# Output parts, key transposes and openings of two cross-attentions put elsewhere in the order of work

## The reference

```python
kv = jnp.concatenate([context, latents], axis=1)   # layer 0; in layer 1 the context alone
q = (latents @ Wq).reshape(bsz, q_len, HEADS, HEAD_DIM).transpose(0, 2, 1, 3)
k = (kv @ Wk).reshape(bsz, kv_len, KV_HEADS, HEAD_DIM).transpose(0, 2, 1, 3)
v = (kv @ Wv).reshape(bsz, kv_len, KV_HEADS, HEAD_DIM).transpose(0, 2, 1, 3)
q = rms_norm(q, q_norm_w)
k = rms_norm(k, k_norm_w)
scores = jnp.einsum('bhgqd,bhkd->bhgqk', qg, k) * scale
probs = jax.nn.softmax(scores.astype(jnp.float32), axis=-1).astype(q.dtype)
...
return out @ Wo
```

## Time and profile before

| | |
|---|---|
| median of 3 runs | 1523.04 us (1520.77 to 1525.49) |
| the profiled execution | 1521.05 us, of which 1519.3 us are the span of the trace |
| mean granted clock of TensorE | 0.984 |
| busy: TensorE, VectorE, ScalarE, GpSimd | 1434.1 us (94%), 1013.1 (67%), 844.4 (56%), 413.2 (27%) |
| median time of a wo tile's load (1024 KB in 16) | 4.9 us |

### The profile page before, as it was taken

The page is one execution under the profiler, slowest core; times in us unless marked ns, Lnnn a source line. Parts: engine busy times, 40 slices in busy tenths (PEclk is TensorE's granted clock), DMA queues, the critical chain, the costliest instruction groups (busy, mean ns, idle before and its releaser), DMA issues.

```text
span 1519.3 us, 23906 instructions
## 1 busy us (share of the span) xinstructions
PE 1434.1 (94%) x7942; PEld 1204.3 (79%) x7942; DVE 1013.1 (67%) x1833; ACT 844.4 (56%) x1476; POOL 413.2 (27%) x570
## 2 busy tenths in 40 slices
PE   8989999988999999779999999999899999978998
PEld 6857888877888888669777788887788888756887
DVE  6778788777666667538667655567656556737765
ACT  5755767664555556426446455556555555733443
POOL 3565445432223221005126222223112222001000
PEclk9999999999999999989999999999999999989999
DMA  8455444553434343246253434344234334423242
GB/s 284 147 201 193 142 181 149 209 187 94 135 120 141 114 154 117 83 145 205 82 193 136 145 119 134 129 153 152 98 118 132 127 129 145 140 78 104 84 166 97
DMA packets 65518, 215.14 MB, mean 142 GB/s; under 512 B 16976, under 2 KB 21840, under 8 KB 58160
## 3 DMA queue, kind: packets, MB, share of 16 engines
q1 hardware_dynamic: 65424, 213.95, 41.3%
HBM read 180.76 MB, written 33.16 MB: 141 GB/s over the span
## 4 chain that ended last, share of the span: by engine, by line
PE 78%; DVE 9%; POOL 3%; ACT 3%; issue 3%; DMA 3%; SPq 0%; DVEq 0%; POOLq 0%; ACTq 0%
PE g_kbanks L54 11%; PE g_kbanks L56 11%; PE g_kbanks L55 11%; PE g_pobanks L1744 7%; PE g_vbank L54 5%; PE g_vbank L55 4%; PE g_vbank L56 4%; PE g_ktbank L1756 4%; PE g_pobanks L1730 3%; PE g_sbank L1712 3%; PE g_sbank L54 2%; PE g_sbank L55 2%; PE g_sbank L56 2%; PE g_pobanks L54 1%; DVE c_wkv_r L215 1%
## 5 line engine op out<-in xcount | busy, mean ns | idle before, releaser
L54 PE MATMUL g_kbanks<-c_wkv_r,c_cT_r 128*128 128x512 f32 x768 | 318.6, 415 | 31.4 <-DVE c_wkv_r L475 16.1
L56 PE MATMUL g_kbanks<-c_wkv_r,c_cT_r 128*128 128x512 f32 x768 | 307.4, 400 | 0.0
L55 PE MATMUL g_kbanks<-c_wkv_r,c_cT_r 128*128 128x512 f32 x768 | 307.2, 400 | 0.0
L54 PEld LDWEIGHTS g_kbanks<-c_wkv_r,c_cT_r 128*128 128x128 f32 x768 | 148.1, 193 | 64.0 <-issue 17.0
L56 PEld LDWEIGHTS g_kbanks<-c_wkv_r,c_cT_r 128*128 128x128 f32 x768 | 147.6, 192 | 34.2
L55 PEld LDWEIGHTS g_kbanks<-c_wkv_r,c_cT_r 128*128 128x128 f32 x768 | 148.0, 193 | 27.5
L1627 POOL TENSOR_TENSOR c1a_ms<-c1a_ss,c_const 128x4 f32<-128x4 f32 x64 | 12.9, 201 | 350.1 <-DVE c1a_ss L2035 350.1
L54 PE MATMUL g_vbank<-c_wkv_r,c_cT_r 128*128 128x512 f32 x256 | 100.7, 393 | 0.6 <-DVE c0a_v L2090 0.6
L55 PE MATMUL g_vbank<-c_wkv_r,c_cT_r 128*128 128x512 f32 x256 | 100.9, 394 | 0.0
L56 PE MATMUL g_vbank<-c_wkv_r,c_cT_r 128*128 128x512 f32 x256 | 100.6, 393 | 0.0
L2041 DVE TENSOR_TENSOR c0a_kn<-c0a_kn,c0a_rstd 128x512 f32<-128x512 f32 x64 | 68.8, 1074 | 47.0 <-POOL c0a_rstd L1630 47.0
(11 more groups left out here) (541 smaller groups left out, 3805.9 us busy)
## 6 DMA issues: line engine op xcount, KB each, us to landing
c_cT_r<-ctx_split_dram SPq DMA_DIRECT2D x48, 1024.0 KB, 5.5
c_cT_r<-ctx_split_dram SPq DMA_DIRECT2D x48, 768.0 KB, 4.8
ctx_split_dram<-c_cT_r SPq DMA_DIRECT2D x16, 1792.0 KB, 7.0
c_wkv<-in_l_wo SPq DMA_DIRECT2D x16, 1024.0 KB, 4.9
g_stage<-in_l_wq SPq DMA_DIRECT2D x15, 1024.0 KB, 5.2
e_stage<-in_e_w SPq DMA_DIRECT2D x20, 768.0 KB, 4.2
c_wkv<-in_l_wkv SPq DMA_DIRECT2D x16, 512.0 KB, 6.2
c_cT<-in_ctx SPq DMA_DIRECT2D x32, 256.0 KB, 3.1
```

What stands on the lines that cost most here:

```text
L54: nc.tensor.matmul(out, a[0], b[1], start=start, stop=False, skip_group_check=reopen)
L55: nc.tensor.matmul(out, a[0], b[0], start=False, stop=False, skip_group_check=reopen)
L56: return nc.tensor.matmul(out, a[1], b[0], start=False, stop=stop, skip_group_check=reopen)
```

## The change

- **Layer 0's first weights**: the sums and splits move to earlier tiles of the queries stage, T4 is summed before T3, all seven blocks are split there (before, some waited until quad 0), and a low half waits for its own sum alone. In layer 1 VectorE forms T3 at tile 13 (`first_t3`).
- **Key transposes**: `kt(2m-1, 1)` moves from the first short-step group to behind S2 T2, `kt(2m, 0)` from the second group to behind A22 T4. `place_k` and `lo_of_k` follow later in ScalarE's and VectorE's order.
- **Openings**: in the quads of the first unit and quad 2 ScalarE squares the keys behind the keep copy; `root(2m, 0)` comes before the context sums in quad 1; a context low half is made later in quad 0.
- **Finish**: each head has one output part, between the scores and pv; part 7 follows the last transposes, and parts 8 to 15 the last pv. ScalarE divides before it splits, and VectorE splits before `ot_place`.

```diff
-        dve.wait_ge(self.summed, 4)
+        block = self.FIRST[n]
+        dve.wait_ge(self.summed, self.READ_BY[block])
         dve.wait_ge(self.hi_ready, n + 1)
-        self.make_lo(self.FIRST[n], self.low(self.FIRST[n]))
+        self.make_lo(block, self.low(block))
...
-    SUM_AT = [OUTPUTS - 16 + n for n in (8, 9, 11, 12)]
-    HI_AT = [OUTPUTS - 16 + n for n in (9, 11, 13, 13, 14, 15)]
-    LO_AT = [OUTPUTS - 16 + n for n in (13, 14, 15)]
+    SUM_AT = (5, 7, 9, 11) if first else (8, 9, 11)
+    T3_AT = None if first else 13
+    HI_AT = (4, 6, 8, 10, 12, 14, 14) if first else (9, 11, 13, 13, 14, 15)
+    LO_AT = (6, 10, 12, 14, 16, 21, 22) if first else (13, 14, 15)
...
-    LATE = range(6, 7), range(3, 7)
+    LATE = (range(0), range(0)) if tail else (range(6, 7), range(3, 7))
...
+            if is_at(m, 1):
+                root(2 * m, 0)
...
                 score(*scored(u, par, side, False))
-                kt(2 * m - 1, 1)
                 pv(*summed_up(u, par, side, False), loads)
             wait_weights(kvw.T2)
             pe.wait_ge(p1_kept, m + 1)
             product(side, context.S2, kvw.T2, x_bank, False).then_inc(products, 1)
+            if not is_at(m, 0):
+                kt(2 * m - 1, 1)
...
             score(*scored(u, par, side, True))
-            kt(2 * m, 0)
             pv(*summed_up(u, par, side, True), loads)
             wait_weights(kvw.T4)
             pe.wait_ge(u3_kept, m + 1)
             product(side, context.A22, kvw.T4, x_bank, False).then_inc(products, 1)
+            kt(2 * m, 0)
...
                 score(a, UNITS - 1, 1, j)
-                out.product(pe, 2 * j + 3)
+                out.product(pe, j + 3)
                 pv(a - 1, *((UNITS - 1, 1, j - 1) if j else (UNITS - 2, 0, UNIT_H - 1)), loads)
-                out.product(pe, 2 * j + 4)
             p_transpose(LAST + UNIT_H - 1, va_added, PAIRS, zbank)
-            out.product(pe, 2 * UNIT_H + 3)
+            out.product(pe, UNIT_H + 3)
             pv(LAST + UNIT_H - 1, UNITS - 1, 1, UNIT_H - 1, loads)
-            for i in range(2 * UNIT_H + 4, PARTS):
+            for i in range(UNIT_H + 4, PARTS):
...
-            act.wait_ge(ka_added, m + 1)
-            square(2 * m, kn[:, 0, :])
-            if not is_at(m, 0):
-                place_k(2 * m - 1, 3 - 2 * side, par if side else 1 - par, u if side else u - 1)
+            opening = is_at(u, 0) or is_at(m, 2)
+            if not opening:
+                key_square(2 * m, 0, ka_added, m)
                 exponential(x1, k1)
             act.wait_ge(products, made(m, "p6"))
             need(act, va_added, m)
             nc.scalar.activation(keep[:, 0, :], x_bank, ACT.Copy).then_inc(u2_kept, 1)
+            if opening:
+                key_square(2 * m, 0, ka_added, m)
+            if not is_at(m, 0):
+                place_k(2 * m - 1, 3 - 2 * side, par if side else 1 - par, u if side else u - 1)
             divide(x1, k1)
...
-            place_k(2 * m, 2 * side, par, u)
             exponential(x2, k2)
...
+            key_square(2 * m + 1, 1, kb_kept, m)
+            place_k(2 * m, 2 * side, par, u)
             divide(x2, k2)
...
                 pt_copy(LAST + j - 1)
                 exponential(LAST + j, j)
-                out.make_hi(act, 2 * j + 4)
-                out.make_hi(act, 2 * j + 5)
                 divide(LAST + j, j)
-                for i in range(2 * j + 6, 2 * j + 8):
-                    wo.make_hi(act, i)
+                out.make_hi(act, j + 4)
+                wo.make_hi(act, j + 6)
...
                 inverse_sum(a, j)
+                out.make_lo(dve, j + 4)
+                wo.make_lo(dve, j + 6)
                 ot_place(a - 1, *((UNITS - 1, 1, j - 1) if j else (UNITS - 2, 0, UNIT_H - 1)))
-                out.make_lo(dve, 2 * j + 4)
-                out.make_lo(dve, 2 * j + 5)
-                for i in range(2 * j + 6, 2 * j + 8):
-                    wo.make_lo(dve, i)
```

More of the change, by code:

```diff
@@ L1642, in split_queries @@
             pool.wait_ge(q_hi, u + 1)
-            root(n, 0)
+            if not rooted:
+                root(n, 0)
             nc.gpsimd.tensor_tensor(flat(q[1]), mine, as_f32(flat(q[0])),
@@ L1950, in finish @@
             out.make_hi(act, 2)
+            exponential(LAST - 1, UNIT_H - 1)
             out.make_hi(act, 3)
-            exponential(LAST - 1, UNIT_H - 1)
+            divide(LAST - 1, UNIT_H - 1)
             for i in range(4, 6):
                 wo.make_hi(act, i)
-            divide(LAST - 1, UNIT_H - 1)
             for j in range(UNIT_H):
@@ L1966, in finish @@
             pt_copy(LAST + UNIT_H - 1)
-            for i in range(14, 16):
-                wo.make_hi(act, i)
-            out.make_hi(act, 12)
+            for q in range(8, 11):
+                out.make_hi(act, q)
+                if q == 10:
+                    out.make_hi(act, 11)
+                    out.make_hi(act, 12)
+                for i in range(2 * q - 6, 2 * q - 4):
+                    wo.make_hi(act, i)
             for i in range(12, PARTS):
@@ L2065, in quad @@
             total(2 * m, 0)
-            if not is_at(m, 0):
-                if tail and is_at(m, 1):
-                    dve.wait_ge(vl_stored, 32)
-                lo_of_k(2 * m - 1, 3 - 2 * side, par if side else 1 - par)
             inverse_sum(x1, k1)
@@ L2072, in quad @@
             normalise(2 * m, 0)
+            if not is_at(m, 0):
+                lo_of_k(2 * m - 1, 3 - 2 * side, par if side else 1 - par)
             late_split(1)
-            if prepared(hf, m + 1):
+            if prepared(hf, m + 1) and not is_at(m, 0):
                 context.make_lo(dve, *following(hf, b, side), 0)
             if last:
-                for i in range(2):
-                    wo.make_lo(dve, i)
+                wo.make_lo(dve, 0)
             if turning:
@@ L2090, in quad @@
             nc.vector.tensor_tensor(v[:, par, 2 * side + 1, :], zbank[:, :], keep[:, 1, :], ALU.add).then_inc(vb_added, 1)
-            if tail and is_at(m, 0):
-                dve.wait_ge(vl_stored, 32)
-            lo_of_k(2 * m, 2 * side, par)
+            if prepared(hf, m + 1) and is_at(m, 0):
+                context.make_lo(dve, *following(hf, b, side), 0)
             inverse_sum(x2, k2)
             ot_place(*summed_up(u, par, side, True))
+            if last:
+                wo.make_lo(dve, 1)
             if turning:
@@ L2105, in quad @@
             total(2 * m + 1, 1)
+            if tail and is_at(m, 0):
+                dve.wait_ge(vl_stored, 32)
+            lo_of_k(2 * m, 2 * side, par)
             dve.wait_ge(products, made(m, "p3"))
@@ L2112, in quad @@
             if last:
-                for i in range(2, 4):
-                    wo.make_lo(dve, i)
+                wo.make_lo(dve, 2)
         def finish():
@@ L2140, in finish @@
             tail_heads(LAST + UNIT_H - 1, zbank)
-            for i in range(14, 16):
-                wo.make_lo(dve, i)
-            ot_place(LAST + UNIT_H - 1, UNITS - 1, 1, UNIT_H - 1)
+            for q in range(8, 11):
+                out.make_lo(dve, q)
+                if q == 10:
+                    out.make_lo(dve, 11)
+                for i in range(2 * q - 6, 2 * q - 4):
+                    wo.make_lo(dve, i)
+                if q == 8:
+                    ot_place(LAST + UNIT_H - 1, UNITS - 1, 1, UNIT_H - 1)
             out.make_lo(dve, 12)
```

34 lines of the change are left out of this document (19 added, 15 removed).

## The result

The changed kernel takes **1508.66 us** (median of 4 runs, 1506.70 to 1511.63) against 1524.22 (4 runs): a ratio of 0.9903 (95% interval 0.9878 to 0.9929), 15.6 us faster. The forecast was 1485 with a range of 1464 to 1508: the sign was right, the size was not, and the time lies just outside. The profiled run took 1507.46 us with a span of 1505.7; before they were 1521.05 and 1519.3.

What follows compares the result with a forecast made beforehand. TensorE, busy 94%, was taken to bound the steady part, VectorE and ScalarE the finishes' heads; groups +23, openings -9 and -6, turnings -3, finishes -43 gave -38 us, hence 1485 us; range 1464 to 1508.

Steps and rivals of the forecast that it cites:

- Finishes: End of each layer's attention: one output part per head shortens the VectorE and ScalarE chain's heads, -43 us in all.
- Groups: Steady short-step groups: without key transposes TensorE waits for the probabilities' copy and lone transposes cost extra, +23 us.
- After a wait the next load follows some 0.05 sooner than in the stream: Short-step groups: queued loads gain 0.05 us after a wait, a credit taken off each group's price.
- rival A: Lone key transposes between long products are cheap, 0.34 us instead of 0.45: 1472, at best 1459; chance 0.10.
- Openings: Start of each layer's attention and the queries stage: fewer waits for keys and weight halves, -9 and -6 us.
- The kt after the next block product gets 1.4 us more, which covers the small waits: First quads: later key transposes cover small key waits, but not all of the longest, 3.3 us.
- The sums now start earlier ... TensorE waits some 4 us there: Layer 0's last queries tiles: sums at tiles 5 to 11 finish splits before the keys, against some 4 us of waits.
- The low bound of the forecast: Layer 0's opening: only 4 us gained if the conflict with GpSimd merely moves to earlier tiles.
- Turnings: Middle quads: the key wait gains a product of 1.4 us and the rest stays, -3 us (+1 to -5).
- B: Finishes stay bound by VectorE and ScalarE, each only 7 to 8 us shorter: 1513; chance 0.09.
- C: Groups: the probabilities' copy slips behind place_k, up to 0.6 us in each of 120: slower, 1557; chance 0.05.
- D: No change: finish heads stay at 9.1 us, later parts and openings pay for the steady part: 1523; chance 0.03.

Runs made afterwards that it cites:

- E9: Kernel before with the new finish and layer 1's new weight schedule, plus wo's low half made one part earlier in VectorE's gap: 1472.57 us, ratio 0.9656.
- E11: Kernel before with the new finish and layer 1's new weight schedule, but ScalarE's old order, splits ahead of the division: one run, 1472.89 us.
- E2: Kernel before with only the key transposes moved, their copies and low halves with them: 1552.31 us, ratio 1.0188.
- E7: E4 with ScalarE squaring the keys ahead of the keep copy in the openings, as before: one run, 1477.24 us.
- E10: Changed kernel with ScalarE squaring the keys ahead of the keep copy in the openings, as before: 1504.48 us, ratio 0.9872.
- E1: Kernel before with the new finish alone, one output part per head and its order of splits: 1480.59 us, ratio 0.9711.
- E3: Changed kernel with layer 0's weight sums and splits back at their old tiles and in quad 0: 1508.62 us, ratio 0.9901.
- E4: Changed kernel with the key transposes back in the short-step groups from quad 3 on: 1478.22 us, ratio 0.9703.

## Why the prediction was wrong

**Finishes: right.** -43 forecast, -45.1 measured (-22.2 and -22.9, forecast -20.5 and -21.5), no wait of 4.1 on wo's low halves. In layer 0 the waits fell from 18.3 us (84.55 - 66.25) to 2.7, and TensorE's busy time by 6.6 for the same matmuls, since the granted clock rose from 0.90 to 1.00. Of the waits that went, the text had not named the longest, that for the next stage's layer norm (before, 590 to 675 us):

```profile
PE g_pobanks L978 <- DVE m_ln_xn L972: 5.2, 1, 5.2
```

The heads: 5.07 and 5.34, then 6.30 twice, where 5.2 and 6.4 had been counted; VectorE's and ScalarE's chain paces the later ones, as the text said. What it didn't see is that the chain was longer than it had to be (E9, E11).

**Groups: right in mechanism, a term too small.** +23 forecast; the trace has +26.5, E2 +29. The step that was off is "After a wait the next load follows some 0.05 sooner than in the stream". The next long products of the two groups before were

```profile
204.67 0.45 PE L54 MATMUL g_kbanks<-c_wkv_r,c_cT_r 128*128 128x512 f32 x1
...
907.63 0.47 PE L54 MATMUL g_kbanks<-c_wkv_r,c_cT_r 128*128 128x512 f32 x1
```

From the first value load to that product it was 1.07 us in layer 0 in the stream (203.60 to 204.67) and is 1.06 behind the wait (202.68 to 203.74); in layer 1 it was 0.92 (906.71 to 907.63) and is 0.92 (909.82 to 910.74). So the queued loads gain nothing. A group saves 0.22 in layer 0 (2.59 to 2.37 us from the first transpose to the next long product) and 0.18 in layer 1 (2.38 to 2.20), no credit comes on top, and the lone transposes cost the rest: quads grew by 0.42 (15.28 to 15.70) and 0.56 (14.56 to 15.12), so (0.42 + 0.44) / 2 = 0.43 and (0.56 + 0.36) / 2 = 0.46 for four of them. The 0.45 of the earlier trace rows was right, and rival A, cheap transposes, is out. Without the 0.05 the text's own prices are 0.22 and 0.27 a group, +29 for 120 of them, which is what E2 shows. The Trainium skill's issue gap ("TensorE: Matmul & The Clock Gate", section "Back-to-back issue gap"), some 81 ns and so by estimate 0.32 for four, is under both numbers here. The fast end of the forecast's range rested on it in part.

**Openings: wrong, and the main cause of the miss.** -15 forecast, +4.8 measured (the queries stages and the openings of both layers). Two steps failed. The first is "The kt after the next block product gets 1.4 us more, which covers the small waits". It does remove the waits for the keys, but the keys weren't the bound. TensorE's waits in layer 0's opening, in total, times and longest:

```profile
PE g_kbanks L54 <- ACT c0a_keep L1939: 5.9, 2, 5.1
PE g_sbank L1720 <- DVE g_stage_r L2002: 1.5, 1, 1.5
```

Before, it was 4.9 for the keys with 3.3 the longest; now it is 5.9 for the keep copy and 1.5 for a low half that the first scores need. The wait moved to the next name in the same queue of work, behind the context's load. The prediction had named that load ("that one in quad 2 hangs on the context's loads too") and still took most of the wait as a gain. And ScalarE's late square, which it gave no cost at all, costs 2.2 to 2.4 and 1.0 us (E7, E10). E2, with the move alone, has the openings of before to 0.1.

The granted clock has a part in it that the waits don't show. The first row is the opening before, the second the one after, the third a piece of the latter:

```profile
90.54:134.02 43.48, 36.82 (x167) 28.03 (x166) 32.51 (x41) 23.61 (x37) 19.41 (x27) 1.00 0.69 263
93.03:138.49 45.46, 38.10 (x166) 30.02 (x165) 25.80 (x35) 20.66 (x34) 18.84 (x26) 0.92 0.64 242
114.70:121.60 6.90, 4.58 (x13) 3.70 (x14) 3.50 (x4) 3.85 (x6) 4.80 (x5) 0.51 0.20 62
```

TensorE waited 6.7 us before (43.48 - 36.82) and waits 7.4 now, so of the waits nothing was saved. The clock fell to half (0.51) while TensorE waited its 5.1 us for the keep copy, and stayed there until 121.6; the 4.58 us of work in that piece would take half at the full clock, so this costs some 2.3 us. In E10 the waits of the opening are 5.5 us and its clock 0.96: of the 2.4 us between the two, 1.9 are waits. The low clock is not the change's doing alone: E1, whose opening has the code of before, is at 0.96 and takes 44.2 in place of 43.5.

The second is "The sums now start earlier ... TensorE waits some 4 us there". The 4 us are too high to begin with. TensorE's waits for low halves at the end of the stage before (60 to 91 us), then those of the changed kernel (30 to 93):

```profile
PE g_sbank L54 <- DVE c0q_w_lo L161: 2.2, 2, 1.6
...
PE g_sbank L54 <- DVE c0q_w_lo L161: 3.3, 3, 1.8
PE g_vbank L54 <- DVE c0q_w_lo L161: 0.5, 1, 0.5
```

So 2.2 us became 3.8. The sums did go, but to tiles in which VectorE had no slack either. The changed kernel in such a tile:

```profile
46.55 4.55 DVE L161 TENSOR_TENSOR c0q_w_lo<-g_stage,c0q_w_hi 128x1024 fp32r<-128x1024 f32 x2
...
47.14 2.88 POOL L206 TENSOR_TENSOR c_wkv<-c_wkv 128x1024 f32<-128x1024 f32 x1
...
51.16 0.50 PE L54 MATMUL g_vbank<-c0q_w_lo,c0q_xT_hi 128*128 128x512 f32 x1 [0.54 <-DVE c0q_w_lo L161]
...
62.53 2.34 DVE L161 TENSOR_TENSOR c0q_w_lo<-g_stage,c0q_w_hi 128x1024 fp32r<-128x1024 f32 x2
```

A pair of low halves takes 4.55 us beside a GpSimd sum and 2.34 without one; at the end of the stage it had been 4.53. The queries stage grew by 2.5 us, of which up to 0.7 are a piece at half the clock (granted clock 0.98 over the stage) that E4, E7 and E10, with the same weights, don't have at 92.3 to 92.7. The opening got 1.2 back (E3). The low bound of the forecast (a gain of 4, the conflict only moves) named this mechanism and had the wrong sign for it. The Trainium skill's rule that GpSimd and VectorE contend for their SBUF interfaces ("GPSIMD Engine Reference", "1. Specifications") fits these rows, and should have weighed more than the idle share of 19%.

**Turnings:** -3 forecast, +0.3 measured. The eight groups in them carry the groups' price, 2.0 us, so the rest gained 1.7; but by the table they vary by 2 us with the clock for equal code, so no gain can be told. The key wait "5.9 late in layer 1" is 4.6 in the trace.

**The rivals.** B (finish stays bound, 1513) is 4 us from the measured time for a reason that doesn't hold: the finish had all its gain. C (the copy slips behind place_k) didn't come: the copy starts 0.64 after the transposes as before. D's 1523 didn't come either. The sum of the misses is 15 + 4.8 in the openings, 3.3 in the turnings and 3.5 in the groups, less 2.1 in the finishes: 24.5, which is what lies between -38 and -13.6. The ends of the terms as the text gives them (+18 and +33, -11 and -4, -7 and -3, -5 and +1, -52 and -30) add up to 1466 and 1520, not to the 1470 and 1502 that it calls its own range; the measured time lies between the first two.

## What to carry to other kernels

A wait of the bounding engine in an opening names whoever came last, not who sets the pace: before counting it as a gain, ask which transfer or sum the next waiter in line hangs on, and count only down to that. Short steps that cover the latency of a copy cost only what they outlast it by (here some 0.2 of 0.45 us); moved out, they cost their full time less what the gap shrinks. When two engines alternate in a loop, look at which one idles before reordering the other: an earlier result on one is lost if it delays the input of the other. And read the granted clock of a stretch beside its waits: with equal code layer 0's turning took 46.0 us at 0.89 and 48.4 at 0.86.

## What the runs showed of the hardware

A run of eight 128-column matmuls behind a wait costs the wait and no more: from its first weight load to the next long product it takes 1.06 and 0.92 us, against 1.07 and 0.92 in the stream. Four 128-column transposes alone between 512-column products cost 0.43 to 0.46. Two VectorE subtractions of 128x1024 with both inputs in SBUF took 4.55 us beside a GpSimd sum and 2.34 without one. And TensorE's granted clock fell to half during a wait of 5.1 us and stayed there beyond it, to 121.6; the same code's turnings differ by 2 us with the time at half the clock (0.89 and 0.86 over layer 0's), and the same code's opening had 1.00 in one execution and 0.96 in another. What makes it fall in one and not in the other was not found.
